# FFN computes only the expert each image takes, in four one-expert tiles; the next group's stem stands among the batches

## What is computed

```python
scores = softmax(mean(x, axis=1) @ Wg.T)          # x: layer-normed tokens, one row of scores an image
sel = top_k(scores, 1)
h = gelu(einsum('bth,ehf->betf', x, W1) + b1)      # 192 -> 768, three experts
y = einsum('betf,efh->beth', h, W2) + b2           # 768 -> 192
out = einsum('beth,be->bth', y, scores * one_hot(sel, 3))
```

## Time and profile before

| | us |
|---|---|
| median of 3 runs | 564.36 (562.98 to 566.38) |
| the profiled execution | 568.5 |
| its span (first to last instruction) | 566.7 |
| PE busy | 469.8 (83%), mean granted clock 0.90 |
| DVE, ACT, POOL busy | 307.4, 224.9, 156.5 |

### The profile page before, as it was taken

The page is one execution under the profiler, slowest core; times in us unless marked ns, Lnnn a source line. Parts: engine busy times, 40 slices in busy tenths (PEclk is TensorE's granted clock), DMA queues, the critical chain, the costliest instruction groups (busy, mean ns, idle before and its releaser), DMA issues.

```text
span 566.7 us, 7771 instructions
## 1 busy us (share of the span) xinstructions
PE 469.8 (83%) x2637; PEld 348.5 (61%) x2637; DVE 307.4 (54%) x1178; ACT 224.9 (40%) x527; POOL 156.5 (28%) x161
## 2 busy tenths in 40 slices
PE   3987456548983799989988899899888998998797
PEld 2464245426672588746776788467766876776575
DVE  3063048615645758185469972755598748373212
ACT  0621863202252354162543742625436422631321
POOL 3003747200471472000760740006608400000000
PEclk9977857776995569999999999999989999998799
DMA  4629525349972152007750640067504300000000
GB/s 103 144 53 244 161 74 153 91 108 269 262 202 56 33 161 63 0 1 178 206 147 1 186 116 1 1 162 206 159 4 132 108 2 0 1 1 16 0 1 16
DMA packets 59046, 54.17 MB, mean 96 GB/s; under 512 B 44354, under 2 KB 51167, under 8 KB 59007
## 3 DMA queue, kind: packets, MB, share of 16 engines
q1 hardware_dynamic: 49360, 25.32, 18.0%
q0 software_dynamic: 9216, 28.32, 17.6%
q10 hardware_dynamic: 431, 0.03, 0.0%
HBM read 38.60 MB, written 15.06 MB: 95 GB/s over the span
## 4 chain that ended last, share of the span: by engine, by line
PE 62%; DVE 17%; ACT 8%; issue 5%; POOL 3%; SPq 2%; DMA 2%; ACTq 1%; DVEq 0%; POOLq 0%
PE bank L729 11%; PE bank L742 11%; PE bank L556 6%; PE bank L467 6%; PE bank L482 4%; PE bank L653 3%; PE bank L672 3%; PE bank L489 3%; POOL ring L428 3%; ACT h L862 2%; PE bank L615 2%; PE bank L657 2%; SPq L371 2%; PE bank L696 2%; DVE o L1217 2%
## 5 line engine op out<-in xcount | busy, mean ns | idle before, releaser
L428 POOL DMA_INDIRECT ring<-cells,cell x144 | 145.3, 1009 | 258.6 <-DVE corner L1116 116.2
L729 PE MATMUL bank<-xfT,w_up 96*128 96x288 f32 x288 | 84.6, 444 | 2.5 <-ACT hid L993 2.5
L742 PE MATMUL bank<-w_down,hid 128*128 128x192 f32 (+1 forms) x432 | 79.1, 339 | 2.4 <-ACT hid L993 2.4
L742 PEld LDWEIGHTS bank<-w_down,hid 128*128 128x128 f32 (+1 forms) x432 | 62.9, 167 | 15.3 <-ACT hid L993 4.2
L556 PE MATMUL bank<-w_dcn,shared 128*128 128x192 f32 (+1 forms) x288 | 62.1, 365 | 7.3 <-ACT shared L890 7.3
L729 PEld LDWEIGHTS bank<-xfT,w_up 96*128 96x128 f32 x288 | 56.5, 206 | 18.7 <-ACT hid L993 3.9
L993 ACT ACTIVATE hid<-bank,b_up 128x288 f32<-128x288 f32 x72 | 35.4, 500 | 69.5 <-PE bank L729 69.4
L1131 DVE SCALAR_TENSOR_TENSOR bank<-ring,corner,bank 128x96 f32<-128x96 f32 x224 | 52.9, 312 | 16.0 <-ACT bank L881 15.9
L556 PEld LDWEIGHTS bank<-w_dcn,shared 128*128 128x128 f32 (+1 forms) x288 | 47.0, 181 | 21.0 <-ACT shared L890 9.4
L467 PE MATMUL bank<-xt,w_stem 96*96 96x384 f32 x96 | 43.5, 588 | 3.4 <-ACT h L862 3.3
L862 ACT ACTIVATE h<-bank,bn_bias,bn_scale 96x384 f32<-96x384 f32 x48 | 31.3, 667 | 32.3 <-PE bank L467 32.3
(11 more groups left out here) (153 smaller groups left out, 633.0 us busy)
## 6 DMA issues: line engine op xcount, KB each, us to landing
cells<-ring SPq DMA_DIRECT2D x16, 864.0 KB, 9.5
xs<-in_x_dram SPq DMA_DIRECT2D x32, 108.0 KB
ring<-cells,cell POOLq DMA_INDIRECT x144, 3.1
w_up<-in_L_ffn_W_dram SPq DMA_DIRECT2D x2, 864.0 KB, 12.4
w_down<-in_L_ffn_W_dram SPq DMA_DIRECT2D x3, 576.0 KB, 15.6
hid<-in_L_tok_dcn_w_dram SPq DMA_DIRECT2D x1, 1152.0 KB, 8.8
out_dram<-y SPq DMA_DIRECT2D x8, 96.0 KB, 2.0
w_qk<-in_L_attn_W_qkv_dram SPq DMA_DIRECT2D x24, 24.0 KB, 1.8
```

The source lines that it names most:

```text
L428: pool.indirect_dma_start(ring[:, ring_slot(k), j, :], None, table[0:HALF_CELLS, :] if k < EARLY else table, bass.IndirectOffsetOnAxis(ap= ...
L729: mm = pe.matmul(ps[5 + n % 2][:, 0:TOK], w_up[:, kt, e, 128 * f:128 * f + 128], xfT[:, kt, :], start=(kt == 0), stop=(kt == 1))
L742: mm = pe.matmul(down_out(e, t), hid[:, e % 2, f, t0:t0 + n], w_down[:, e, f, :], start=(f == 0), stop=(f == FCH - 1))
```

## The change

Each image's expert is known on the chip only. The change sorts the eight images of a group into four tiles of three places (`SLOT` = 108 tokens), each tile of one expert. Eight images and three experts always fit. The steps are: `wanted` (DVE) makes a one-hot row an image; `ranks` (PE, two small matmuls) counts the images of each expert, before this one and in all; `slots` (DVE, a chain of 13 small operations) works out the first tile of each expert, each image's place and each tile's expert as an integer; `spots` (PE) spreads the place over the tokens; `positions` (DVE) compares it with 0 to 431 and so builds the 0/1 matrix `into` of 288 x 432; `into_slots` (PE, six calls of 432 columns) moves the tokens to their places and turns them; `slots_copy` (ACT). Then for each tile j: `up(j)` reads the expert into a PE register and multiplies the 108 tokens, now stationary, with 384 moving columns of the expert's weights, 4 calls (the bias is a 97th row); `gelus` (2 of 108 x 384); `turn` (six transposes); `turn_copies`; `down` (six calls of 192 columns, again with the register); `y_copy`. `where_by_slot` (PE) and `ways_back` (DVE) build four matrices that bring the rows back, which `back_to_tokens` does (12 calls of 192 columns, and three small ones for the gate); `add_back` (DVE) adds gate times result to the tokens in `h3`, which is now double and stored from directly; `y`, `spread_gates`, `add_expert` and the transposes of `xf` are gone. The gate's exponential moves behind those of the features.

The stem of group g+1 moves: `stem_x` and the first products stand at the start of the step, the others and the pieces of the FFN between the batches (`between`); its `leaky` stand among the combines on DVE; it uses banks 4 and 7 for the products. The images are loaded two groups ahead, and POOL's copies of rows stand in the middle of a gather. Batch 1 is combined in its own step, not in the step before. Five small tables are loaded more at the start, ahead of `ld_attn`; the broadcast of b2 and the transposed b1 go.

The core of the diff (the last group after the loop runs ranks, spots, `where_by_slot`, `into_slots`, up 0, up 1, turn 0, up 2, down 0, turn 1, up 3, down 1, turn 2, down 2, turn 3, down 3, `back_to_tokens`):

```diff
-            sp.dma_start(spread[0:GROUP, 0:TOK], w["spread"]).then_inc(ld_img, 16)
+            sp.dma_start(spread[0:GROUP + 1, 0:TOK], w["spread"]).then_inc(ld_img, 16)
+            sp.dma_start(earlier[:, :], w["before"]).then_inc(ld_img, 16)
+            sp.dma_start(places[:, :], w["places"].partition_broadcast(128)).then_inc(ld_img, 16)
+            sp.dma_start(slotrow[:, :], w["slotrow"]).then_inc(ld_img, 16)
+            sp.dma_start(where[GROUP:GROUP + 1, :], w["ninth"]).then_inc(ld_img, 16)
+            sp.dma_start(y_slot[SLOT:SLOT + EXPERTS, 0, :], w["b2"]).then_inc(ld_img, 16)
             for n, kt in ((n, kt) for n in range(6) for kt in range(2)):
...
+                        rearrange_rows(g + 1)
                     if k >= SLOTS:
...
                     if u >= 2:
                         pe.wait_ge(xt_evac, 6 * g + (u - 1))
+                    elif g >= 2:
+                        pe.wait_ge(y_added, 3 * (g - 2))
...
+            def between(g, k, has_next):
+
+                if has_next:
+                    if k == 0:
+                        spots(g - 1)
+                        stem_products(g + 1, 0, 4, 6)
+                    elif k == 1:
+                        stem_x(g + 1, 1, 0, 1)
+                    elif k == 2:
+                        stem_x(g + 1, 1, 1, 3)
+                    elif k == 3:
+                        stem_products(g + 1, 1, 0, 3)
+                        into_slots(g - 1, 6 * (g + 2))
+                    elif k == 4:
+                        stem_products(g + 1, 1, 3, 6)
+                    elif k == 5:
+                        up(g - 1, 0)
+                    elif k == 6:
+                        pe.wait_ge(bn_evac, 12 * (g + 2))
+                        turn(g - 1, 0)
+                        up(g - 1, 1)
+                    elif k == 7:
+                        down(g - 1, 0)
+                    else:
+                        turn(g - 1, 1)
                 else:
...
-                    if has_last and has_next and k == BATCHES - 1:
-                        stem_x(g + 1, 0, 0, 2)
+                        between(g, k, has_next)
                     dcn_products(g, k)
                 if has_last:
-                    down(g - 1, 1, 1)
-                    down(g - 1, 1, 2)
+                    if has_next:
+                        up(g - 1, 2)
+                    down(g - 1, 1)
...
+            def ranks(g):
+
+                pe.wait_ge(hot_ready, g + 1)
+                pe.wait_ge(y_added, 3 * g)
+                if g + 2 < GROUPS:
...
+            def into_slots(g, evicted):
+                pe.wait_ge(xt_evac, evicted)
+                pe.wait_ge(into_ready, 3 * (g + 1))
+                for m in range(2):
+                    for t, (t0, n) in enumerate(ROWTILES):
+                        mm = pe.matmul(ps[5 + m][0:96, 0:PLACES], xf[0:n, t, 96 * m:96 * m + 96], into[0:n, t, :],
+                                       start=(t == 0), stop=(t == 2))
+                    mm.then_inc(xs_mm, 1)
...
+                if j == 0:
+                    pe.wait_ge(xs_evac, 2 * (g + 1))
+                else:
+                    pe.wait_ge(gelu_done, 8 * g + 2 * j)
+                chosen[j] = pe.value_load(expert[0:1, j:j + 1], min_val=0, max_val=EXPERTS - 1)
+                for half in range(2):
+                    for kt, rows in ((0, 96), (1, 97)):
+                        mm = pe.matmul(ps[5 + half][0:SLOT, 0:HALF_FF], xs_slots[0:rows, kt, SLOT * j:SLOT * (j + 1)],
+                                       w_up[0:rows, kt, chosen[j], HALF_FF * half:HALF_FF * (half + 1)],
                                        start=(kt == 0), stop=(kt == 1))
                     mm.then_inc(up_mm, 1)
 
...
+            def turn(g, j):
+                if 4 * g + j >= 1:
+                    pe.wait_ge(y_evac, 4 * g + j)
+                for half in range(2):
+                    pe.wait_ge(gelu_done, 8 * g + 2 * j + half + 1)
+                    for f in range(FCH // 2):
+                        mm = pe.transpose(ps[TURN_BANKS[half]][:, SLOT * f:SLOT * (f + 1)], hid_tok[:, half, 128 * f:128 * f + 128],
+                                          ident[0:SLOT, 0:SLOT])
+                    mm.then_inc(turn_mm, 1)
+
...
+            def down(g, j):
+                pe.wait_ge(turn_evac, 8 * g + 2 * j + 2)
                 for f in range(FCH):
...
+            def where_by_slot(g):
+                if g < GROUPS - 1:
+                    pe.wait_ge(gelu_done, 8 * g + 6)
+                pe.matmul(where_bank(g)[0:SLOT + EXPERTS, 0:TOK], where[:, :], spread[0:GROUP + 1, 0:TOK],
+                          start=True, stop=True).then_inc(where_mm, 1)
...
+                for t, (t0, n) in enumerate(ROWTILES):
+                    pe.matmul(ps[6][0:n, 256 + t:257 + t], spread[0:GROUP, t0:t0 + n], gatev[:, :], start=True, stop=True)
+                pe.wait_ge(y_evac, 4 * (g + 1))
+                pe.wait_ge(back_ready, 4 * (g + 1))
+                for t, (t0, n) in enumerate(ROWTILES):
+                    for j in range(FFN_TILES):
+                        rows = SLOT + EXPERTS if j == 0 else SLOT
+                        mm = pe.matmul(returned(t), back[0:rows, j, t0:t0 + n], y_slot[0:rows, j, :],
+                                       start=(j == 0), stop=(j == FFN_TILES - 1))
+                    mm.then_inc(ret_mm, 1)
 
 
             pe.wait_ge(ld_stem, 48)
...
             def step(g, has_last, has_next):
-                if has_last:
+                if has_last and has_next:
+                    stem_x(g + 1, 0)
+                    logits(g - 1)
+                    stem_products(g + 1, 0, 0, 2)
+                    ranks(g - 1)
+                    stem_products(g + 1, 0, 2, 4)
+                elif has_last:
...
+                else:
+                    turn(g - 1, 2)
+                if has_last:
+                    down(g - 1, 2)
                 channels(g, xn, xn_ready, t2_mm, ROWTILES)
                 if has_next:
                     offsets_by_token(g + 1)
                 qkv(g, has_next)
+                if has_last:
+                    where_by_slot(g - 1)
                 features(g)
                 kv_sums(g)
                 attend(g)
                 if has_last:
-                    up(g - 1, 2, 0, 1)
+                    pe.wait_ge(back_ready, 4 * g)
+                    up(g - 1, 3)
                 channels(g, xa, xa_ready, t3_mm, TILES)
                 if has_last:
-                    up(g - 1, 2, 1, 1)
+                    turn(g - 1, 3)
+                    pe.wait_ge(turn_evac, 8 * g)
                 project(g)
                 if has_last:
...
+            def gelus(g, j):
+                for half in range(2):
+                    n = 8 * g + 2 * j + half
+                    act.wait_ge(up_mm, n + 1)
+                    if n >= 2:
+                        act.wait_ge(turn_mm, n - 1)
+                    act.activation(hid_tok[:, half, :], ps[5 + half][0:SLOT, 0:HALF_FF], ACT.Gelu).then_inc(gelu_done, 1)
...
+                else:
+                    turn_copies(g - 1, 2)
+                if has_last:
+                    y_copy(g - 1, 2)
                 copy_banks(g, t2_mm, lnT, t2_evac)
                 squares(g)
                 exps(g)
+                if has_last:
+                    prob_exps(g - 1)
                 kv_high(g)
                 outputs_first(g)
+                if has_last:
+                    gelus(g - 1, 3)
                 copy_banks(g, t3_mm, lnT, t3_evac)
                 if has_last:
-                    gelus(g - 1, 2)
...
+            def positions(g):
+                dve.wait_ge(posn_mm, g + 1)
+                chain = Chain(dve, posn_chain, g, 2)
+                chain.add(dve.tensor_copy(posn[:, 0:FULL], ps[5][:, 8:8 + FULL]))
+                chain.link(dve.tensor_copy(posn[0:REST, FULL:], ps[5][0:REST, 8 + FULL:9 + FULL]))
+                if later(g):
+                    dve.wait_ge(ret_mm, 3 * g)
...
-                    ins = dve.tensor_copy(gates[0:n, t, :], ps[4][0:n, 4 * t:4 * t + 3])
-                ins.then_inc(gates_ready, 1)
-                dve.wait_ge(gates_ready, g + 1)
-
...
+            def add_back(g):
+                dve.wait_ge(ret_mm, 3 * (g + 1))
+                dve.tensor_copy(gates[:, 0:FULL], ps[6][:, 256:256 + FULL])
+                dve.tensor_copy(gates[0:REST, FULL:], ps[6][0:REST, 256 + FULL:257 + FULL]).then_inc(gate_copied, 1)
+                dve.wait_ge(gate_copied, g + 1)
+                h3 = residual(g)
+                for t, (t0, n) in enumerate(ROWTILES):
+                    dve.scalar_tensor_tensor(h3[0:n, t, :], returned(t)[0:n, :], gates[0:n, t:t + 1], h3[0:n, t, :],
+                                             ALU.mult, ALU.add).then_inc(y_added, 1)
 
...
             def step(g, has_last, has_next):
                 if has_last:
-                    gate_logits(g - 1)
-                    combine(g, 2, 3)
-                    gate(g - 1)
```

(15 more changed lines are left out.)

490 lines of the change are left out of this document (288 added, 202 removed).

## The result

The changed kernel takes 595.07 us (median of 4 runs, 591.41 to 597.54) against 563.96 us (4 runs, 562.98 to 566.38): a ratio of 1.054, with a 95% interval of 1.046 to 1.062. The direction was forecast and the time lies in the stated range (556 to 602), but above the 568 to 590 us of the forecast itself: 580.7 us, +16.3, was expected, where +31.1 came. The profiled execution of after took 597.54 us (span 595.5), 29.0 more than that of before; it is the longest of its four, the others are 0.2 to 6.1 us shorter.

A forecast was written before the change was run, and what follows sets the result against it. Bound in turn by dense PE work, short PE-ACT-DVE chains and the norm on DVE. Start 2.2, step 1 -1.4, step 2 2.6, step 3 6.0, tail 2.1, register 4.8: +16.3 on 564.4, median 580.7 us; range 556 to 602.

The forecast's parts named there:

- Sum of PE work: TensorE work per group falls from 36.6 to 30.6 us, 24 us in all, counting only where PE finishes last.
- Start: Before the first step: five more small loads ahead of the attention weights, 0.43 us an issue, +2.2 us.
- Step 1: From group 0's second norm done to group 1's: stem rows 7.8 us earlier, 6.4 given back, -1.4 us.
- Step 2: From group 1's second norm done to group 2's: stem gains 5.8, waits cost 6.4, half clock 2, +2.6 us.
- Step 3: From group 2's second norm done to group 3's: no next stem fills gaps; 1.5 us for the clock included, +6.0 us.
- Tail: From the last group's second norm to the end: a chain with one tile in flight, 56.0 against 53.9 us, +2.1.
- Register: Reading each tile's expert into a PE register: 0.30 us for each of 16 tiles, +4.8 us, ends 0 and 29.
- The first: Rival: PE work is what counts, so the 24 us saved come through; 542 us, or 553 with half; chance 0.17.
- the second: Rival: gains and givebacks cancel, register and clock cost nothing; +5.5, or 565 us with 5 us fewer waits; chance 0.08.
- The third: Rival: register read costs 1.2 us a tile, and half clock lasts 21 us in steps 2 and 3; 599 us; chance 0.15.
- The fourth: Rival: stem rows arrive too late to stand among the batches, PE waits at `stem_x`; 592 us; chance 0.03.
- The clock in all: Half-clock allowances after idling: 2 us in step 2, 1.5 in step 3, 2.5 in the tail.

The follow-up runs named there:

- the experiment: For the 6.6 us: the changed kernel with the next group's stem behind the nine batches again, 610.5 us; for 4.5 and 0.1 us: the first experiment.
- the first experiment: The changed kernel plus matmuls nobody reads in TensorE's idle stretches at the start of the steps and in the tail: 582.3 us (1.030).
- early reads: The changed kernel with all four experts of a group read into registers right behind the placing, not one ahead of each tile: 595.3 us (1.059).

## Why the prediction was right or wrong, step by step

**Sum of PE work.** Right: 24 us forecast, about 23 by busy time times clock; and right that it doesn't shorten the kernel. The sign named for it was wrong: busy time itself fell by 2.3 us and not by 24, as the clock fell too.

**Start, +2.2.** Wrong, +0.7 in all. The attention loads' last issue came 0.21 us later than in the earlier trace rows (120.85 us), PE went on at 127.72 instead of 127.64. I priced each added load by one issue of 0.43 us, but SP began the row of loads 1.6 us earlier and took 0.35 us for each of the five.

**Step 1, -1.4 and reads.** Right in sign and size: -0.6; `stem_rows` begins 58.0 us after the cut (246.07), where 57.7 was laid out.

**Step 2, +2.6 and reads.** The gain of the stem's place was right (6.6 us by the experiment, 5.8 laid out). `stem_rows` begins 59.5 us after the cut, where 54.8 was laid out and the earlier trace rows has 60.6; with the clock up in the first experiment it begins at 55.0. The step that failed is the half clock: I took 2 us between the ends 0 and 4.4, on the reason that PE was busy for most of the time. It was busy and stayed at 0.50 for 20 us, and that cost 4.5 us by the experiment: the upper end. The gap ahead of `stem_x` has the releaser that was named (L1527 is in `add_back`), but 1.93 us and not 3.

**Step 3, +6.0 and reads.** Measured +9.8, and not for the reason taken: the clock's 1.5 us are not there (0.1 by the experiment, in which the clock rose, but only to 0.63, 0.84 and 0.85 in the first 30 us), and the layout was short instead. The placing began 21.8 us after the cut (20.4 laid out); from there to the transposes of xn went 35.3 us (32.2 laid out); after them 3.6 us came on top of before (2.75 laid out). Among the terms the placing is visibly too cheap: 4.4 us by the bare pace of the columns, 5.0 at full clock in the trace of step 2 and 6.1, partly at half clock, in step 3. The rest of the 3.1 us isn't traced to a term.

**Tail, +2.1 and reads.** The largest miss, +13.3. The clock's share is an estimate: 49.07 us busy at 0.73, so 13.2 us. Less that, the tail is 54.0 us, and less the 2.8 of the register reads 51.2, where 53.5 was laid out with 2.5 us for the clock taken off: the layout of the chain was some 2 us too long. The failed step is that 2.5, "five of its us at half clock", for a tail whose clock was 0.50 to 0.67 in its first 36 us. It was taken from one window of before, where the tail had dense work behind it. Part of this miss is the draw of the profiled execution: the same tail took 59.5 us at 0.84 in another kernel, so a tail of after can be 7.7 us shorter, and even then it is 2.3 us over the forecast.

**Register, +4.8.** Right in the total (3.8 measured, with ends 0 and 29), wrong in its make-up: 0.30 a tile was a mean of 0.7 us exposed, in the tail (2.8 us in all by the waits), and nearly nothing in the steps (with a fixed expert they are 0.2 us shorter, 0.8 longer and 1.2 shorter). That the total came out near was luck.

**Rivals.** The first (work counts) fell, as did the second (gains and givebacks cancel). The third had two halves: no read costs 1.2 us, but its other half, the half clock through the first 21 us of steps 2 and 3, is what the trace shows, at 4.5 and 0 us where it priced 4 for both on top. Its 599 us is closer to the 595 measured than the forecast is, and its sign came as well: the tail's up products stand behind waits of 1.31 to 2.13 us, of which only 0.6 to 0.7 us is the read. The fourth fell: the stem stands among the batches.

**The clock in all:** 6 us forecast (2, 1.5, 2.5); 4.5, 0 and 13.2 measured. That is 11.7 of the 12.5 us by which the span was missed; the rest (start -1.5, step 1 -0.4, step 3's layout +4.1, the tail's layout -2.3 and its reads +1.6, and others) nearly cancels. The 13.2 is of the profiled execution, the longest.

## What to carry to other kernels

Leaving out work on an engine can cost more than it saves when the work was also what kept it from idling and at full clock: lay out the critical chain with the stretch behind each new gap at half clock, and take the upper end where that engine has work all along (step 2: 8.0 and 10.0 of 10 us busy, 4.5 us lost); where another engine's work beside it ends last anyway, nothing is lost (step 3: 6.9 and 6.1 busy, 0.1 us). Where a tile's steps go through three engines, give it a second set of banks: it was worth 9.8 us in a tail of 59.5, 6.8 of them waits. Read registers behind queued matmuls, not behind a wait.

## What the runs showed of the hardware that was not expected

- The granted clock stayed at 0.50 for 20 us with PE busy 9.93 and 10.00 of 10.00 us (step 1 of after), so busy time in a profile doesn't tell the clock. The Trainium skill (TensorE: Matmul & The Clock Gate, What's actually happening) has the clock follow how busy the array has recently been; these rows don't show that from the busy time alone.
- Six unread matmuls of 128 columns (2.9 us there) behind `route` went with 0.71 and 1.00 in the first 20 us of step 1 instead of 0.50 and 0.50. The twenty at the start of step 2 went with 0.83 and 1.00 in one kernel and with 0.63 and 0.50 in another.
- The same tail took 67.2 or 59.5 us by its clock (0.73 or 0.84). At nearly full clock in the tail four runs agreed within 0.07 us.
- A read of a register from SBUF on PE costs about 0.7 us where PE stands waiting for its data (2.02 us against 1.41 ahead of up(2)), and nothing visible behind 5 us and more of queued matmuls (early reads).
- On two of the four chips of the experiments the kernel of before took 17 to 18% longer. Versions that share all but one or two moves with one that was 1.7% slower than before elsewhere were 1.4 and 2.1% faster than it there.
